# A fused attention and expert layer kernel: the statistics of batches 4 to 7 and the second table move ahead of the first expert tile, and the third weight waits for batch 0

## The chip, the cores and the metric

The kernel runs on one core of one Trainium2 chip. The metric is the device time of one execution in microseconds. Three runs of the kernel before gave 274.36, 274.52 and 274.54 us, a median of 274.52 us.

## The reference, cut to what matters

Two residual layers follow one another on x, 8 batches of 512 tokens with 128 features. The first is a mixing layer with a scan over the tokens, the second a layer of 8 experts of which each token takes 2.

```python
# layer 1
n = layernorm(x)                                  # per token, over 128 features
inp = mix * n + (1 - mix) * shifted(n)            # shifted by one token in the batch
h = relu(inp @ W_in.T + b_in)
state = state * decay + h_t                       # over the 512 tokens of a batch
x = x + layernorm(states @ W_out.T + b_out)
# layer 2
n = layernorm(x)
weights, chosen = top_k(n @ gate_kernel, 2); weights = softmax(weights)
# for each of the two (token, expert) pairs, weights w0, w1 (128 x 512), wo (512 x 128):
y = (silu(n @ w0[e]) * (n @ w1[e])) @ wo[e]
x = x + layernorm(sum of the two weighted y)
```

## The kernel before, in words

The program is written out by hand, one instruction stream for each engine, with semaphores between them; the order in each function is the order on that engine, and each engine and each DMA queue works in order. Times below are counted from the start of the profiled span.

**The head.** Batches 0, 1, 2 (and the first part of 3) go through layer 1 before the first expert tile. For batch b: `start1(b)` takes mean and variance of the raw x on DVE (`bn_stats` L953, `bn_aggr` L937), `root1(b)` the square root on ACT, `scale_z(b)` scales the projected rows on DVE; `mix_and_turn(b)` and `times_folded(b)` are matmuls, `relu(b)` is on ACT (L686), `scan(b)` on DVE (L1001), `times_w_out(b)` on PE (L1710 and L1715). `squares2(b)` and `root2(b)` on ACT give the second normalisation, `residual(b)` (L1016) on DVE the new x. Then `top`, `choice` and `choose` pick the experts on DVE, `squares(b)` and `root3(b)` on ACT and `offset3(b)` on DVE normalise, `ranks(b)` on PE and `put(b)`, `tags(b)` on DVE work out where each row goes. `normalise3(b)` on ACT (L699) writes the rows, and POOL sends them into the `expert_rows` table in DRAM by eight indirect DMAs for a batch (L524). `s_sent[0]` counts the landings of batch 0's eight.

**Tables.** `table_start(p)`, `table_end(p)`, `use_tiles(p)` on DVE make the list of tiles of phase p from the counts of the batches so far. Phase 0 holds tiles 0 to 2, phase 1 tiles 3 to 7, phase 2 tiles 8 to 15. SP loads the rows of the tiles (L370) once the table of the phase is there and the sends of its batches have landed; phase 0 needs batch 0 and the first two sends of batch 1.

**Slots.** From there one loop `for k, s, t in slots()` runs on PE, ACT, DVE and POOL. PE's slot t turns the rows of tile t (L1759), does the first two layers of tile t-1 (L1764, 16 matmul records) and the last layer of tile t-2 (L1801, 8 records). ACT copies the turned rows (L743), applies silu (L748), copies w0 for the next tile (L766) and scales the result (L777). DVE multiplies into `sb_gated` (L1368) and copies w1 for the next tile (L1387). POOL sends results to `pair_rows` (L537). The layer 1 work of batches 3 to 7 is spread over the slots; a batch takes eight. The function `batch_at(t, ahead)` says which.

**What the change touches in the slots.** Before, batches 5 to 7 get their statistics in the slots: four `bn_stats` each in DVE's slots 5, 6, 7 (`rest_sums`, L983), twelve `bn_aggr` in slot 8 (`rest_mean_var`, L990), then `rest_power` on POOL in slot 8 (two operations, L487 and L491) and `rest_means` on ACT in slot 9 (L639), which waits for the `bn_aggr`. Batch 4's are in DVE's head (`start1(4)`, after `tags(2)`). The table of phase 1 is made in DVE's slots 0 to 2, that of phase 2 in slots 2 to 4.

**SP's queue** holds in order: the loads of x and its turned copy, `load_w(0)`, `load_w(1)` (2 MB each, L340), `load_x(4, 4, B)` (1 MB, L336), the load of wo (2 MB, L362), then the tile loads. All of these travel in one DMA queue.

**Fills.** `fill(bank, n)` issues n bf16 matmuls of 128x512 (L1810) whose result nobody reads; the kernel before has them at the very start and just ahead of tile 0.

## Time and profile before

| | |
|---|---|
| median of three runs | 274.52 us (274.36 to 274.54) |
| the profiled execution's own time | 274.19 us |
| its span | 272.4 us, so 1.8 us lie around it |
| PE busy | 243.0 us, 89% |
| DVE, ACT, POOL busy | 68%, 66%, 61% |
| mean granted TensorE clock | 0.964 of full speed |

The profile was taken in one execution. A row of the timeline has the start, the duration, the engine, the line, what is written from what, how many instructions were merged into it, and in square brackets the idle time of the engine just before it with what ended it. Matmuls overlap in their pipeline, so durations of neighbours overlap.

### The profile page before, as it was taken

Reading aid. Unit: us, or ns where it says so; the run is one execution under the profiler, and the core shown is the slowest. Engines: PE = TensorE matmul, PEld = TensorE weight load, DVE = VectorE, ACT = ScalarE, POOL = GpSimd, SP = SyncE. Lnnn points to the kernel's source line nnn. Section 1 sums busy time; section 2 is a strip of 40 time slices with the busy share of each in tenths; the row PEclk is TensorE's granted clock in tenths of the full one; section 3 lists DMA queues with packets and bytes.
Section 4 is the critical chain, followed back from the end, with each engine's and each line's share of the span. In section 5 each row is a group of like instructions: output and inputs, shape, how many; then the busy total and the mean of one; then the engine's idle time right before and its main releaser. Section 6 shows DMA issues by size and latency. Waiting matters only on the chain.

```text
span 272.4 us, 8097 instructions
## 1 busy us (share of the span) xinstructions
PE 243.0 (89%) x2059; PEld 231.2 (85%) x2059; DVE 186.1 (68%) x815; ACT 179.0 (66%) x517; POOL 167.2 (61%) x190
## 2 busy tenths in 40 slices
PE   7948778899898999999999999999999999999800
PEld 2738655799898999999999999999999999999700
DVE  4886876877785785687578687844353434998774
ACT  2185869577576777785867587655656566568581
POOL 3317774773678878778878878776333324277740
PEclk9997799999999999999999999999999999999955
DMA  5999961413301321132123113433322108403048
GB/s 174 300 358 375 292 215 51 101 52 84 106 32 49 88 84 40 62 96 65 40 71 101 49 45 108 110 90 89 82 78 70 51 28 331 178 16 96 13 152 231
DMA packets 29675, 31.70 MB, mean 116 GB/s; under 512 B 4778, under 2 KB 22188, under 8 KB 29504
## 3 DMA queue, kind: packets, MB, share of 16 engines
q1 hardware_dynamic: 24448, 22.56, 27.7%
q0 software_dynamic: 4320, 8.50, 8.9%
q8 instruction: 19, 0.31, 0.5%
q10 hardware_dynamic: 864, 0.13, 0.3%
q14 instruction: 24, 0.20, 0.2%
HBM read 19.58 MB, written 12.05 MB: 116 GB/s over the span
## 4 chain that ended last, share of the span: by engine, by line
PE 73%; DVE 14%; issue 4%; POOL 4%; ACT 2%; DVEq 1%; POOLq 0%
PE bank L1764 40%; PE bank L1801 21%; PE bank L1715 3%; PE bank L1759 2%; DVE sb_early L1001 2%; PE bank L1810 2%; PE bank L1665 1%; POOL expert_rows L524 1%; ACT sb_square L653 1%; DVE sb_w_now L1387 1%; DVEq L1381 1%; DVE sb_rest_stats L983 1%; PE bank L1683 1%; POOL pair_rows L537 1%; DVE sb_x L1016 1%
## 5 line engine op out<-in xcount | busy, mean ns | idle before, releaser
L1764 PE MATMUL bank<-sb_xeT,sb_w_now 128*128 128x128 f32 x1136 | 139.5, 275 | 2.9 <-DVE sb_gated L1368 2.4
L1764 PEld LDWEIGHTS bank<-sb_xeT,sb_w_now 128*128 128x128 f32 x1136 | 133.0, 192 | 3.8 <-issue 3.8
L537 POOL DMA_INDIRECT pair_rows<-sb_y_rows,sb_y_pair x71 | 73.4, 1033 | 53.3 <-ACT sb_y_rows L777 32.3
L1368 DVE TENSOR_TENSOR sb_gated<-bank,sb_silu 128x512 f32<-128x512 f32 x71 | 48.9, 689 | 58.0 <-PE bank L1764 46.8
L524 POOL DMA_INDIRECT expert_rows<-sb_row,sb_place x64 | 64.8, 1012 | 28.9 <-issue 18.1
L1801 PE MATMUL bank<-sb_w_raw,sb_gated 128*128 x568 | 75.7, 276 | 0.4 <-ACT sb_y_rows L777 0.3
L1801 PEld LDWEIGHTS bank<-sb_w_raw,sb_gated 128*128 128x128 f32 x568 | 69.1, 192 | 1.0 <-issue 0.9
L748 ACT ACTIVATE sb_silu<-bank 128x512 f32<-128x512 f32 x71 | 42.3, 595 | 17.2 <-PE bank L1764 16.9
L743 ACT ACTIVATE sb_xeT<-bank 128x128 f32<-128x128 f32 x71 | 19.4, 274 | 40.8 <-PE bank L1759 40.5
L766 ACT ACTIVATE sb_w_now<-sb_w_raw 128x512 f32 x71 | 44.3, 624 | 0.0
L1387 DVE COPY sb_w_now<-sb_w_raw 128x512 f32 x71 | 30.2, 425 | 1.6 <-issue 1.6
L777 ACT ACTIVATE sb_y_rows<-bank,sb_y_weight 128x128 f32<-128x128 f32 x71 | 25.7, 361 | 2.0 <-PE bank L1801 1.8
L1759 PE MATMUL bank<-sb_ident_wide,sb_taken_rows 128*128 128x128 f32 x71 | 19.6, 277 | 1.4 <-ACT sb_xeT L743 1.0
L699 ACT ACTIVATE sb_row<-sb_x,sb_nm,sb_rs 128x128 f32<-128x128 f32 x32 | 14.1, 484 | 1.0 <-DVE sb_nm L1028 1.0
L1715 PE MATMUL bank<-sb_w_out_wide,sb_early 128*128 128x136 f32 x64 | 11.3, 328 | 2.7 <-DVE sb_early L1001 2.6
L1715 PEld LDWEIGHTS bank<-sb_w_out_wide,sb_early 128*128 128x128 f32 x64 | 9.6, 223 | 4.4 <-DVE sb_early L1001 4.2
L1016 DVE SCALAR_TENSOR_TENSOR sb_x<-bank,sb_rs,sb_x 128x136 f32<-128x136 f32 x32 | 9.3, 352 | 5.0 <-POOL sb_rs L482 4.9
L1759 PEld LDWEIGHTS bank<-sb_ident_wide,sb_taken_rows 128*128 128x128 f32 x71 | 10.1, 143 | 2.3 <-ACT sb_xeT L743 1.5
L482 POOL TENSOR_TENSOR sb_rs<-sb_sd,sb_minus_half 128x4 f32<-128x4 f32 x10 | 11.2, 1120 | 0.8
L1665 PE MATMUL bank<-sb_wide,sb_pairs_early 128*128 128x136 f32 x64 | 10.4, 314 | 0.0
L1665 PEld LDWEIGHTS bank<-sb_wide,sb_pairs_early 128*128 128x128 f32 x64 | 9.7, 225 | 0.7 <-ACT sb_wide L605 0.7
L1810 PE MATMUL bank<-sb_ones_b 128*128 128x512 bf16 x22 | 7.6, 495 | 2.6 <-POOL sb_pad_row L461 1.8
(203 smaller groups left out, 249.8 us busy)
## 6 DMA issues: line engine op xcount, KB each, us to landing
sb_taken_rows<-expert_rows SPq DMA_DIRECT2D x71, 65.5 KB, 1.9
sb_w_raw<-in_L_ffn_w SPq DMA_DIRECT2D x2, 2048.0 KB, 16.2
sb_pairs_early<-pair_rows SPq DMA_DIRECT2D x3, 1024.0 KB, 7.2
...
pair_rows<-sb_y_rows,sb_y_pair POOLq DMA_INDIRECT x71, 2.4
...
```

What stands on the lines that cost most here:

```text
L524: pool.indirect_dma_start(expert_rows[:, :], bass.IndirectOffsetOnAxis(ap=place[b % ROWS][:, k, j:j + 1], axis=0), row[b % ROWS][:, j, :], ...
L537: pool.indirect_dma_start(pair_rows[:, :], bass.IndirectOffsetOnAxis(ap=y_pair[group % 2][:, t % PAIRS:t % PAIRS + 1], axis=0), y_rows[slo ...
L748: act.activation(silu[t % 2][:], p_l1[:], ACT.Silu).then_inc(c["silu"], 1)
L766: act.activation(w0_now[t % 2][:].rearrange("p (c f) -> p c f", f=D), w_raw_chunks[:, bass.ds(chunks[t], FC), :], ACT.Copy).then_inc(c["w0 ...
L777: act.activation(y_rows[t % Y_SLOTS][:], p_y[t % 2][:, 0:D], ACT.Copy, scale=y_weight[group % 2][:, t % PAIRS:t % PAIRS + 1]).then_inc(c[" ...
L1368: dve.tensor_tensor(gated[t % 2][:], p_l2[:], silu[t % 2][:], ALU.mult).then_inc(c["gated"], 1)
L1387: dve.tensor_copy(w1_now[t % 2][:].rearrange("p (c f) -> p c f", f=D), w_raw_chunks[:, bass.ds(chunks[t] + W_CHUNKS, FC), :]).then_inc(c[" ...
L1665: last = pe.matmul(p_z(b)[h][:, j * Z_WIDE:(j + 1) * Z_WIDE], x_turned[:, at:at + P], wide[:, D:], start=True, stop=True)
L1715: last = pe.matmul(p_attn(b, j), states[b % 2][:, j * P:(j + 1) * P], w_out_wide[:], start=False, stop=(j % (G // 2) == 1))
L1759: pe.transpose(p_xeT, taken_rows[:, t % RING, 0:D], ident).then_inc(c["xeT_ps"], 1)
L1764: last = pe.matmul(to[:, n * P:(n + 1) * P], w[:, n * P:(n + 1) * P], x, start=True, stop=True)
L1801: last = pe.matmul(p_y[t % 2][:, 0:D], gated[t % 2][:, n * P:(n + 1) * P], wo.rearrange("p o d -> p (o d)"), start=(n == 0), stop=(n == FC ...
```

## The change

The load of x for batches 4 to 7 goes ahead of w0 and w1. SP's load of wo waits until all of batch 0's sends have landed. On DVE, `scan(0)` goes ahead of `start1(1)`, `start1(4)` moves up to between `choose(1)` and `offset3(1)`, all statistics of batches 5 to 7 and batch 4's inverse root move ahead of `residual(2)`, and the table of phase 1 is made whole ahead of the slots. The inverse roots of batches 5 to 7 are made by a square root on ACT and a reciprocal on DVE in place of POOL's two operations. ACT's order is changed around tile 0, and PE gets fills in three more places of the head.

```diff
@@ sync
             load_turned(4, 4, B)
+            load_x(4, 4, B)
             load_w(0, w0_in)
             load_w(1, w1_in)
-            load_x(4, 4, B)
+            sp.wait_ge(s_sent[0], 16 * K * G)
             sp.dma_start(w_raw[:, 2 * WCOLS:].rearrange("p (e c n) -> p e c n", e=E, c=FC),
...
@@ gpsimd
-            def rest_power():
...
-                if t == STEP:
-                    rest_power()
@@ scalar
+            def rest_root():
+                act.wait_ge(rest["mv"], 1)
+                act.activation(rest_sd[:], rest_mv[:, :, 1], ACT.Sqrt,
+                               bias=eps[:]).then_inc(rest["sd"], 1)
...
             root2(1)
             keep_z(3)
+            mean_of_x(2)
+            mean_of_x(3)
             relu(2)
...
-            mean_of_x(2)
+            root1(4)
+            mean_of_x(4)
             squares2(2)
             root2(2)
             keep_z(6)
-            relu(3)
+            keep_z(7)
+            chunk_of(0)
+            fetch_w0(0)
+            rest_root()
             squares(2, 0, G)
             root3(2)
-            keep_z(7)
-            root1(4)
-            mean_of_x(3)
-            mean_of_x(4)
             act.activation(unused[:], eps[:], ACT.Silu)
-            chunk_of(0)
-            fetch_w0(0)
+            relu(3)
+            normalise3(2, 0, G // 2)
...
                 if t == 0:
-                    normalise3(2, 0, G)
+                    normalise3(2, G // 2, G)
@@ vector
+            def rest_inverse():
+                dve.wait_ge(rest["sd"], 1)
+                dve.reciprocal(rest_rs[:], rest_sd[:]).then_inc(rest["rs"], 1)
...
             decays()
-            start1(1)
             folded_weights()
             scan(0)
+            start1(1)
...
             choose(1)
+            start1(4)
             offset3(1)
...
             use_tiles(0)
+            rest_sums(0, (B - REST) * G)
+            rest_mean_var()
+            inverse(1, 4, REST, sd1, rs1)
             residual(2)
             top(2)
             choice(2)
             choose(2)
+            rest_inverse()
             offset3(2)
             put(2)
             tags(2)
-            start1(4)
-            inverse(1, 4, REST, sd1, rs1)
             chunk_of(0)
             fetch_w1(0)
+            table_start(1)
+            table_end(1)
+            use_tiles(1)
 
             for k, s, t in slots():
-                if t == 0:
-                    table_start(1)
-                elif t == 1:
-                    table_end(1)
-                elif t == 2:
-                    use_tiles(1)
+                if t == 1:
                     table_start(2)
...
-                if t in (STEP - 3, STEP - 2, STEP - 1):
-                    rest_sums((t - STEP + 3) * G, (t - STEP + 4) * G)
-                elif t == STEP:
-                    rest_mean_var()
@@ tensor
             times_folded(2)
+            fill(bank[4], 6)
             ranks(0)
+            pe.wait_ge(a["hidden"], 2)
+            fill(bank[5], 5)
             times_w_out(1)
...
             times_folded(5)
+            pe.wait_ge(a["hidden"], 3)
+            fill(bank[5], 4)
             times_w_out(2)
             times_folded(6)
+            times_folded(7)
             mix_and_turn(3)
-            times_folded(7)
             ranks(2)
```

**SP, at the loads of x and the weights**, as a difference between the two orders. The first two rows are loads of the turned x, the row with `in_L_ffn_w` the two weights.

```order
 L345 DMA sb_pairs_early<-in_x_turned 128x512
 L345 DMA sb_pairs_early<-in_x_turned 128x2048
+L336 DMA sb_x<-in_L_attn_x 128x16x128
 L340 DMA sb_w_raw<-in_L_ffn_w 128x8x512 x2
-L336 DMA sb_x<-in_L_attn_x 128x16x128
```

The 1 MB of x now stands ahead of 4 MB of weights, and behind them comes wo with its new wait.

**DVE, between the end of `use_tiles(0)` and the choice of batch 2**, before:

```order
L1176 TENSOR_TENSOR sb_used<-sb_used,sb_take 128x8
L945 RECIPROCAL sb_rs_0<-sb_sd_0 128x4
L1016 SCALAR_TENSOR_TENSOR sb_x<-bank,sb_rs_0,sb_x 128x136 x4
L1036 MAX sb_top_0<-sb_x 128x8 x4
L1043 MAX_INDEX sb_choice_0<-sb_top_0,sb_x 128x8 x4
```

and with the change:

```order
L1178 TENSOR_TENSOR sb_used<-sb_used,sb_take 128x8
L979 BN_STATS sb_rest_stats<-sb_x 128x6 x12
L986 BN_AGGR sb_rest_mv<-sb_rest_stats 128x2 x12
L941 RECIPROCAL sb_rs_4<-sb_sd_4 128x4
L941 RECIPROCAL sb_rs_0<-sb_sd_0 128x4
L1018 SCALAR_TENSOR_TENSOR sb_x<-bank,sb_rs_0,sb_x 128x136 x4
L1038 MAX sb_top_0<-sb_x 128x8 x4
L1045 MAX_INDEX sb_choice_0<-sb_top_0,sb_x 128x8 x4
```

Twenty-four statistics and a reciprocal now stand ahead of `residual(2)`.

**DVE, from the w1 copy of tile 0 to the first product**, with the change (the six rows of `table_start` and five of `table_end` and the three of `use_tiles`, L1172 to L1178, stand above this piece):

```order
L1178 TENSOR_TENSOR sb_used<-sb_used,sb_take 128x8
L1383 TENSOR_LOAD sb_tile_chunk_i
L1383 ISA x2
L1389 ISA
L1389 COPY sb_w_now<-sb_w_raw 128x512
L1003 SCALAR_TENSOR_TENSOR sb_early<-sb_decay_row,sb_early 128x512
L1119 TENSOR_SCALAR sb_tiles_i<-sb_count_i 128x8
L1123 TENSOR_SCALAR sb_full<-sb_tiles_i 128x8
L1126 TENSOR_TENSOR sb_avail<-sb_full,sb_used 128x8
L1131 SCALAR_TENSOR_TENSOR sb_ends<-sb_ones_f,sb_avail 128x8
L1136 SCALAR_TENSOR_TENSOR sb_skip<-sb_used,sb_full 128x8
L1140 TENSOR_TENSOR sb_past<-sb_tile_f,sb_ends 128x8x8
```

Between the scan of batch 3 (L1003) and tile 0's product stands now the start of the table of phase 2; before it was the end of the table of phase 1.

## Rows read from the trace of the kernel before

**Rows 1.** Busy time by stretch: PE, PEld, DVE, ACT, POOL, then clock, DMA share, GB/s.

```profile
47.40:74.90 27.50, 25.19 (x218) 24.08 (x218) 21.50 (x106) 17.50 (x51) 17.39 (x20) 1.00 0.33 87
74.90:99.40 24.50, 23.60 (x212) 23.08 (x211) 17.67 (x75) 18.73 (x55) 19.76 (x21) 1.00 0.22 65
99.40:123.70 24.30, 24.30 (x223) 24.21 (x223) 17.39 (x76) 18.29 (x54) 19.45 (x21) 1.00 0.23 67
```

**Rows 2.** Timeline of PE, 50 to 86.5 us: the rows with an idle time before them.

```profile
50.83 1.13 PE L1764 MATMUL bank<-sb_xeT,sb_w_now 128*128 128x128 f32 x8 [0.52 <-ACT sb_silu L748]
52.75 1.13 PE L1764 MATMUL bank<-sb_xeT,sb_w_now 128*128 128x128 f32 x8 [0.79 <-DVE sb_gated L1368]
...
68.59 1.13 PE L1764 MATMUL bank<-sb_xeT,sb_w_now 128*128 128x128 f32 x8 [0.69 <-DVE sb_gated L1368]
74.33 1.15 PE L1801 MATMUL bank<-sb_w_raw,sb_gated 128*128 x8 [0.30 <-ACT sb_y_rows L777]
...
85.99 0.68 PE L1764 MATMUL bank<-sb_xeT,sb_w_now 128*128 128x128 f32 x4 [0.90 <-DVE sb_gated L1368]
```

**Rows 3.** Groups by line on DVE and POOL, 60 to 76 us: the moved and removed work.

```profile
L983 DVE BATCH_NORM_STATS2 sb_rest_stats<-sb_x 128x6 f32<-128x128 f32 x12 | 2.6, 275 | 0.0
L990 DVE BATCH_NORM_AGGREGATE sb_rest_mv<-sb_rest_stats 128x2 f32<-128x6 f32 x12 | 0.9, 148 | 0.0
...
L491 POOL TENSOR_TENSOR sb_rest_rs<-sb_rest_sd,sb_minus_half 128x12 f32<-128x12 f32 x1 | 2.3, 2297 | 0.1
```

**Rows 4.** Timeline of DVE, the start of the head.

```profile
9.41 0.87 DVE L953 BATCH_NORM_STATS2 sb_stats<-sb_x 128x6 f32<-128x128 f32 x4
10.42 0.38 DVE L937 BATCH_NORM_AGGREGATE sb_mv<-sb_stats 128x2 f32<-128x6 f32 x4
...
15.32 0.36 DVE L1016 SCALAR_TENSOR_TENSOR sb_x<-bank,sb_rs,sb_x 128x136 f32<-128x136 f32 x1
```

**Rows 5.** Timeline of PE, 9 to 43 us.

```profile
10.00 1.09 PE L1665 MATMUL bank<-sb_wide,sb_pairs_early 128*128 128x136 f32 x8
...
12.37 1.19 PE L1715 MATMUL bank<-sb_w_out_wide,sb_early 128*128 128x136 f32 x8
...
20.93 2.18 PE L1715 MATMUL bank<-sb_w_out_wide,sb_early 128*128 128x136 f32 x8 [1.60 <-DVE sb_early L1001]
...
42.09 0.33 PE L1759 MATMUL bank<-sb_ident_wide,sb_taken_rows 128*128 128x128 f32 x1 [0.36 <-DMA sb_taken_rows<-expert_rows]
```

**Rows 6.** Busy time by stretch in the head, columns as in rows 1.

```profile
17.50:20.90 3.40, 0.76 (x9) 0.42 (x9) 3.06 (x18) 3.02 (x12) 0.08 (x1) 0.99 1.03 396
20.90:24.30 3.40, 3.37 (x15) 3.37 (x16) 1.94 (x11) 1.48 (x10) 2.79 (x3) 0.51 1.05 390
```

**Rows 7.** Timeline of DVE, 27 to 52 us: the rows that end a wait, and the products.

```profile
28.88 0.18 DVE L945 RECIPROCAL sb_rs<-sb_sd 128x4 f32<-128x4 f32 x1 [0.81 <-ACT sb_sd L629]
34.64 0.18 DVE L945 RECIPROCAL sb_rs<-sb_sd 128x4 f32<-128x4 f32 x1 [0.67 <-ACT sb_sd L624]
38.80 0.18 DVE L945 RECIPROCAL sb_rs<-sb_sd 128x4 f32<-128x4 f32 x1 [0.76 <-ACT sb_sd L629]
41.43 0.18 DVE L945 RECIPROCAL sb_rs<-sb_sd 128x4 f32<-128x4 f32 x1 [0.37 <-ACT sb_sd L600]
42.67 0.43 DVE L1387 COPY sb_w_now<-sb_w_raw 128x512 f32 x1 [1.06 <-issue]
47.32 0.69 DVE L1368 TENSOR_TENSOR sb_gated<-bank,sb_silu 128x512 f32<-128x512 f32 x1 [0.44 <-issue]
51.91 0.69 DVE L1368 TENSOR_TENSOR sb_gated<-bank,sb_silu 128x512 f32<-128x512 f32 x1 [0.51 <-issue]
```

**Rows 8.** Issues of SP from the timeline: start, time in the issue.

```profile
18.88 8.60 SPq L362 DMA_DIRECT2D sb_w_raw<-in_L_ffn_wo  x1
...
39.06 2.62 SPq L370 DMA_DIRECT2D sb_taken_rows<-expert_rows  x3
```

**Rows 9.** The sends (L524): landing times of the eight issued from 20 to 31 us.

```profile
DMA to landing us min/median/max: 5.8/6.4/7.2
```

12 lines of the change are left out of this document (3 added, 9 removed).

## The prediction

> **What bounds the kernel now.** I read the page's busy shares first (in the table above): PE is the engine to watch, at 89%. Then the busy time by stretch [rows 1]. From 99.4 to 123.7 us, a batch period of eight tiles, PE is busy for all of its 24.3 us: from there to the end of the tiles the matmuls alone set the pace, and nothing the change does can be felt. The period before it has 0.9 us in which PE does nothing (24.50 less 23.60), and the stretch from the first product at 47.4 us has 2.3 (27.50 less 25.19). The timeline of PE names these gaps [rows 2]: 0.52 and 0.79 us at 51 and 53 us, 0.69 at 69, 0.30 at 74 and 0.90 at 86. They add up to 3.2 us, and that is all there is to win in the slots. Anything else must come out of the head, and the head can be judged by one moment: when PE can start the second half of tile 2's layers, at 52.75 us, released by DVE's product of tile 1 at 51.91 us [rows 2, 7].
>
> **What the change wins in the slots.** The gaps at 69 and 74 us lie in slots 7 to 9, where DVE does the twelve `bn_stats` and `bn_aggr` (2.6 and 0.9 us) and ACT waits for them. The gap at 86 us hangs on POOL: its power of 12 columns takes 2.3 us [rows 3] and pushes the sends of batch 3 and, behind them, the inverse root that `residual(4)` needs. With all of this gone, these slots hold what the later periods hold, and there PE has no gap [rows 1]. I take the three as won whole: 0.69 + 0.30 + 0.90 = **1.89 us**. The gaps at 51 and 53 us belong to the first tiles and go into the next sum.
>
> **What it costs in the head.** I follow DVE, step by step, as shifts against the times of before.
>
> First, `start1(1)` behind `scan(0)`. `start1(1)` fills a time, from 9.41 us on, in which DVE waits for the folded weights from PE anyway; now DVE stands idle there and ends the scan about half a microsecond earlier, near 11.8 us. PE gets next to nothing from it, since the projections of batch 1 hold it until 10.00 + 1.09 us and the bias product follows [rows 5]. But `start1(1)` (0.87 + 0.38 us, with the pause between them 1.39) [rows 4], its round trip over ACT, the scaling and `start1(2)` now stand in one row between the scan and `residual(0)`. I add them up to 16.1 us for that residual, which was at 15.32 [rows 4]: batch 0 comes **0.8 us later**, and POOL's first send with it.
>
> Second, the fills. From 17.5 to 20.9 us PE is busy for 0.76 of 3.40 us, and in the stretch behind the granted clock is 0.51, the 1.2 GHz level [rows 6]; there the eight `times_w_out(1)` records take 2.18 us, against 1.19 us for batch 0's at 2.4 GHz [rows 5]. The change puts 11 fills around `ranks(0)`, all in time in which PE would wait for DVE, so they cost nothing themselves. If the clock stays up, 0.99 us come back: batch 1's residual is then **0.2 us earlier** than before. The same happened again at 31 us, but behind the new order nothing waits for batch 2's product.
>
> The Trainium skill, "TensorE: Matmul & The Clock Gate", Part 1, says the array sits at 1.2 GHz after idleness and gets 2.4 GHz only after sustained activity; the rows of these two stretches agree with it. The rule also speaks against this change, since it makes PE idle elsewhere.
>
> For with `ranks(2)` late, PE idles from about 36.3 to 41.3 us, ahead of the ten fills of tile 0, and these may run at 1.2 GHz as the stretch at 20.9 us did. That costs nothing in my sum as long as the first two layers end before 50 us, so I take 0. The other end is the price of the one stretch at 1.2 GHz above, 1.0 us.
>
> Third, `start1(4)`, 1.4 us, ahead of `offset3(1)`. DVE waits there for 0.81 us anyway [rows 7]; so batch 2's scan and the first table come **0.2 us later** than before.
>
> Fourth, the statistics of batches 5 to 7 ahead of `residual(2)`: 2.6 + 0.9 us [rows 3], 0.2 for the pause and the inverse root, 3.7 us in all. Before, DVE waited 0.67 us there [rows 7]. `residual(2)` comes 0.2 + 3.7 - 0.7 = **3.2 us later**, near 38 us.
>
> Fifth, what is no longer behind it: the wait of 0.76 us for ACT at 38.80 (`relu(3)` no longer stands ahead of `squares(2)`), `start1(4)` with 1.4, and its wait of 0.37 us [rows 7]. The reciprocal of 12 columns adds 0.2. The w1 copy of tile 0 comes 3.2 - 0.8 - 1.4 - 0.4 + 0.2 = 0.8 to 0.9 us later than 42.67.
>
> Sixth, the tables. The end of the table of phase 1 and its `use_tiles` (1.5 us) now stand ahead of `scan(3)`, and the start of the next table (1.1 us) ahead of tile 0's product. So that product is late by much more, 2.7 us, near 50.0 us in place of 47.32. But the same operations are gone from between the products of tiles 0 and 1, and tile 1's comes only **1.0 us late**, at 52.9 us. The sum of operations on DVE up to there is the same; only the added statistics and the waits count.
>
> **The DMA side costs nothing in my sum.** The queue moves 396 GB/s under load [rows 6]. The 1 MB of x, now first, takes 3 us of that and lands well before DVE asks for it at 28 us; all 5 MB take 13 us from about 8 us on, and even at half the rate w1 would be there at 35 us, while it is wanted at 43. Batch 0's last send goes out near 32.4 us. The sends took 5.8 to 7.2 us to land with the weights in the way [rows 9]. Now the way may be clear, so wo starts between 33 and 39 us; I take 36. Its 2 MB take 5.3 us and a start of some 2 us. Tile 0's load, issued at 39.06 us before [rows 8] and there at 42.09 [rows 5], stands behind wo on SP and in its queue, so its rows come near 44 to 45 us. From there PE needs the turn of 0.33 us [rows 5], a copy on ACT, and two layers of about 1.0 us each [rows 2], some 2.6 us. DVE isn't ready before 50 us, so there is room for 2.5 us.
>
> **The sum.** 1.0 us lost, 1.89 won: 0.9 us less. The profiled execution took 274.19 us (span 272.4 and 1.8 around it) and would take 273.3. The median of the runs shown is 0.33 above that execution, so I forecast **273.6 us**.
>
> **The rivals.** *The head is not longer.* DVE is idle for a good part of the time from 34 to 52 us, also in the issue of its register loads (1.06, 0.44 and 0.51 us in [rows 7]), and the added 3.7 us may fall into more of it than I found. Then the product of tile 1 is at 51.9 us as before and the slots' gain stands alone: 274.52 - 1.89 = 272.6 us. For it: the chain has many short waits, and I counted four. Against: each was followed, and the additions stand in the row itself.
>
> *The clock falls all the same.* The fills leave about 1.7 us of idle time before `ranks(0)`. Then the 2.18 us stay, the 0.8 us of batch 0's delay go through, and tile 1 is 2.0 us late: 274.52 - 0.91 + 0.99 = 274.6 us, no change. Against it: PE would be busy for about twice the share that it has now.
>
> *Tile 0 waits for its rows, slower.* Place: SP, behind the load of wo. That issue held SP for 8.60 us [rows 8]. If batch 0's sends still land 6.4 us after their issue, near 38.3 us, and the issue of wo again holds the queue for 8.6 us, tile 0's load goes out at 46.9 us, its rows come 3.0 us later as now (39.06 to 42.09), and the first product is at 52.6 instead of 50.0. That is 274.52 - 0.91 + 2.6 = 276.2 us. It decides once the load's issue is later than 50.0 - 2.6 - 3.0 = 44.4 us. Against: the 8.60 us were spent with three loads queued ahead; now none is.
>
> The Trainium skill speaks for this rival. Its page "DMA: Bandwidth & Descriptors", Queues, rings and completion order, says that within a queue descriptors are taken in order, and that each engine takes turns between queues: the sends, in another queue, are then never shut out by wo, while tile 0's load is. If the wait wins nothing by that rule, the time is that of this rival or of my forecast.
>
> **How the numbers follow.** A measurement of this kernel can tell about 0.2%, 0.55 us, from no change; "faster" is below 273.97, "slower" above 275.07. Forecast (272.9 to 274.4): 0.42, three quarters of it on the fast side. Longer head absent, 272.6: 0.30. Clock falls, 274.6: 0.13, almost all within 0.2%. Rows late, 276.2, with milder forms: 0.15. Together 0.61 faster, 0.22 the same, 0.17 slower. The range 272.0 to 275.3 takes in the first three with 0.6 to 0.7 us on either side of them (most of the 1.0 us of slow fills among it) and leaves out the last.
>
> **What would show it.** Right: no gap on PE from 54 to 100 us, the stretch of tiles 9 to 16 fully busy; tile 1's product near 52.9 us; `residual(2)` near 38 us; a clock of 1.0 at 20.9 to 24.3 us; tile 0's rows landing before 47 us. Wrong: a tile load issued after 44.4 us with PE waiting on a DMA; `residual(0)` not later than 15.5 us; or gaps that stay at 69 and 86 us, which would mean that others than the moved operations caused them.

## The result, and the profile after

| | before | after |
|---|---|---|
| median of the runs, us | 274.53 (274.36 to 274.75, 4 runs) | 271.49 (270.91 to 272.23, 4 runs) |
| ratio to before | 1 | 0.989, 95% interval 0.9869 to 0.9912 |
| profiled execution, us | 274.19 | 272.23 |
| its span, us | 272.4 | 270.5 |
| product of tile 0 / 1 / 2 / 8 / 16, us | 47.32 / 51.91 / 54.78 / 74.88 / 99.31 | 50.07 / 52.87 / 55.71 / 72.94 / 97.24 |

The change takes 3.0 us off; the forecast was 0.9, and 271.49 lies below the range that I gave (272.0). The profiled executions differ by less than the medians, 1.96 us, because that of before was shorter than all the four runs beside it, and that of after the longest of its four. Of all runs reported below, three of e12_split_stats, its profiled one among them, lie more than 1.5% above its fastest; its ratio and median leave them out.

I start with DVE, on which my sum for the head was made. Timeline of DVE in the changed kernel; the columns are start, time, instruction, and in brackets the idle time before it with its releaser.

```profile
16.02 1.16 DVE L1018 SCALAR_TENSOR_TENSOR sb_x<-bank,sb_rs,sb_x 128x136 f32<-128x136 f32 x4
...
25.47 1.16 DVE L1018 SCALAR_TENSOR_TENSOR sb_x<-bank,sb_rs,sb_x 128x136 f32<-128x136 f32 x4
...
34.87 2.40 DVE L979 BATCH_NORM_STATS2 sb_rest_stats<-sb_x 128x6 f32<-128x128 f32 x12
37.31 0.91 DVE L986 BATCH_NORM_AGGREGATE sb_rest_mv<-sb_rest_stats 128x2 f32<-128x6 f32 x12
38.52 1.16 DVE L1018 SCALAR_TENSOR_TENSOR sb_x<-bank,sb_rs,sb_x 128x136 f32<-128x136 f32 x4
...
43.75 0.43 DVE L1389 COPY sb_w_now<-sb_w_raw 128x512 f32 x1 [0.75 <-issue]
...
50.07 0.69 DVE L1370 TENSOR_TENSOR sb_gated<-bank,sb_silu 128x512 f32<-128x512 f32 x1 [0.49 <-issue]
...
52.87 0.69 DVE L1370 TENSOR_TENSOR sb_gated<-bank,sb_silu 128x512 f32<-128x512 f32 x1 [0.45 <-PE bank L1763]
```

The residuals of batches 0, 1 and 2 stand at 16.02, 25.47 and 38.52 us (I had 16.1, 24.6 and about 38), the products of tiles 0 and 1 at 50.07 and 52.87 (50.0 and 52.9). The head ended where I had it. One thing is new: tile 1's product is released by PE (L1763), where in the kernel before DVE itself was late [rows 7].

Busy time by stretch, from tile 0's product to tile 8's, to tile 16's, to tile 24's; columns as in [rows 1].

```profile
50.10:73.00 22.90, 22.90 (x211) 22.81 (x210) 16.93 (x73) 17.55 (x51) 15.03 (x16) 1.00 0.32 88
73.00:97.30 24.30, 24.30 (x223) 24.21 (x222) 17.55 (x75) 18.42 (x54) 19.45 (x21) 1.00 0.22 65
97.30:121.60 24.30, 24.30 (x223) 24.21 (x222) 17.57 (x76) 18.43 (x55) 19.45 (x21) 1.00 0.25 68
```

PE has no gap left in the first two stretches. The first eight tiles take 22.9 us where they took 27.5, the next eight 24.3 where they took 24.5 [rows 1]: 4.8 us won behind tile 0's product, against 2.75 us lost ahead of it.

The granted clock of the head, by stretch of the same view:

```profile
16.30:19.70 3.40, 1.36 (x13) 0.58 (x12) 2.90 (x22) 2.16 (x12) 0.00 (x0) 1.00 1.00 303
19.70:23.10 3.40, 3.40 (x13) 1.96 (x13) 3.09 (x16) 2.24 (x7) 1.27 (x2) 0.50 1.04 393
...
29.90:33.30 3.40, 3.40 (x14) 2.15 (x13) 3.23 (x18) 3.03 (x10) 2.79 (x3) 0.50 0.16 53
...
40.20:43.60 3.40, 1.83 (x11) 0.92 (x12) 2.27 (x20) 3.34 (x11) 1.96 (x3) 0.50 1.04 323
43.60:47.00 3.40, 3.40 (x10) 1.24 (x8) 2.43 (x15) 1.19 (x5) 1.62 (x2) 0.50 0.45 115
```

Here I was wrong: despite the fills the clock went to the 1.2 GHz level at 19.7 us, as it had at 20.9 [rows 6], again from 29.9, and again from 40.2 to 47.0. The timeline of PE shows what that did ahead of tile 0:

```profile
41.77 0.19 PE L1725 MATMUL bank<-sb_taken,sb_ones_b 128*128 128x8 bf16 x1 [4.50 <-DVE sb_taken L1064]
...
42.18 4.43 PE L1809 MATMUL bank<-sb_ones_b 128*128 128x512 bf16 x10
46.40 0.42 PE L1758 MATMUL bank<-sb_ident_wide,sb_taken_rows 128*128 128x128 f32 x1
...
47.47 1.95 PE L1763 MATMUL bank<-sb_xeT,sb_w_now 128*128 128x128 f32 x16
```

The ten fills took 4.43 us; tile 0's turn followed at 46.40, its two layers ran at 2.4 GHz from 47.47 to 49.42. That is hardly before DVE was ready: where PE sets the product of tile 0 (e3 and e6 below) it starts 0.11 us after the layers end, so here PE would have allowed it at 49.5 us, and DVE took it at 50.07.

### The profile page after: what moved, and what is told of

The parts are those of the page before. It is cut to its first block, busy times and chain, and to the rows that moved or that the text cites. A ratio compares the mean times of both kernels' runs of the same rounds, so it can differ in the third digit from the quotient of the medians.

```text
span 270.5 us, 8129 instructions
## 1 busy us (share of the span) xinstructions
PE 245.0 (91%) x2074; PEld 231.1 (85%) x2074; DVE 186.3 (69%) x816; ACT 179.2 (66%) x518; POOL 167.1 (62%) x188
## 4 chain that ended last, share of the span: by engine, by line
PE 81%; DVE 13%; issue 2%; ACT 1%; POOL 1%; DVEq 0%; POOLq 0%
PE bank L1763 45%; PE bank L1800 23%; PE bank L1809 4%; PE bank L1758 3%; PE bank L1714 2%; DVE sb_x L1018 1%; DVE sb_stats L949 1%; DVE sb_early L1003 1%; DVE sb_rest_stats L979 1%; DVE sb_choice L1045 1%; DVE sb_x L1469 1%; PE bank L1690 1%; DVE sb_early L1459 1%; PE bank L1709 1%; DVE sb_x L961 1%
## 5 line engine op out<-in xcount | busy, mean ns | idle before, releaser
L1763 PE MATMUL bank<-sb_xeT,sb_w_now 128*128 128x128 f32 x1136 | 138.7, 275 | 0.2 <-DVE sb_gated L1370 0.2
L1763 PEld LDWEIGHTS bank<-sb_xeT,sb_w_now 128*128 128x128 f32 x1136 | 132.8, 192 | 0.4 <-issue 0.4
L528 POOL DMA_INDIRECT pair_rows<-sb_y_rows,sb_y_pair x71 | 74.7, 1052 | 54.2 <-ACT sb_y_rows L771 34.6
L737 ACT ACTIVATE sb_xeT<-bank 128x128 f32<-128x128 f32 x71 | 19.5, 275 | 46.1 <-PE bank L1758 45.8
L1758 PE MATMUL bank<-sb_ident_wide,sb_taken_rows 128*128 128x128 f32 x71 | 19.7, 277 | 0.0
L1809 PE MATMUL bank<-sb_ones_b 128*128 128x512 bf16 x37 | 15.3, 574 | 1.8 <-POOL sb_pad_row L462 1.8
L1809 PEld LDWEIGHTS bank<-sb_ones_b 128*128 128x128 bf16 x37 | 4.7, 134 | 7.9 <-issue 5.5
L1714 PE MATMUL bank<-sb_w_out_wide,sb_early 128*128 128x136 f32 x64 | 9.7, 299 | 0.0
L1003 DVE TENSOR_TENSOR_SCAN sb_early<-sb_decay_row,sb_early 128x512 f32<-128x512 f32 x8 | 9.7, 1214 | 0.0
```

The costliest lines, as they stand in the source:

```text
L528: pool.indirect_dma_start(pair_rows[:, :], bass.IndirectOffsetOnAxis(ap=y_pair[group % 2][:, t % PAIRS:t % PAIRS + 1], axis=0), y_rows[slo ...
L1714: last = pe.matmul(p_attn(b, j), states[b % 2][:, j * P:(j + 1) * P], w_out_wide[:], start=False, stop=(j % (G // 2) == 1))
L1758: pe.transpose(p_xeT, taken_rows[:, t % RING, 0:D], ident).then_inc(c["xeT_ps"], 1)
L1763: last = pe.matmul(to[:, n * P:(n + 1) * P], w[:, n * P:(n + 1) * P], x, start=True, stop=True)
L1809: pe.matmul(bank[:], ones_b[:], ones_b[:, None, :].broadcast_to([P, FC, P]), start=True, stop=True)
```

## The experiments

The experiments are fifteen variants and a repetition of the changed kernel, on four chips, with runs of the kernel before on the same chip. Across chips the ratio is the measure, since the median of before was 275.07 us on the first (e1 to e4), 274.45 on the second (e5 to e8), 274.57 on the third (e9, e11, e12, e14) and 274.23 on the fourth (after_again, e10, e13, e15). "P0", "P2" and "P16" are the starts of the products of tiles 0, 2 and 16 in the profiled execution, from the timeline of DVE. P0 says how long the head was, P0 to P2 what the first table did in the slots, and P2 to P16 what the statistics did. The 5.97 us of e3, e7 and e8 in P0 to P2 go with a low clock in tile 0's layers.

| kernel | median | ratio (95%) | P0 | P0 to P2 | P2 to P16 |
|---|---|---|---|---|---|
| before | 274.53 | 1 | 47.32 | 7.46 | 44.53 |
| after | 271.49 | 0.9890 (0.9869 to 0.9912) | 50.07 | 5.64 | 41.53 |
| after_again | 271.37 | 0.9899 (0.9874 to 0.9923) | 49.65 | 5.64 | 41.42 |
| e1_no_fills | 272.65 | 0.9902 (0.9868 to 0.9936) | 51.53 | 5.64 | 41.51 |
| e2_wo_at_once | 271.23 | 0.9851 (0.9808 to 0.9894) | 49.73 | 5.63 | 41.44 |
| e3_stats_in_slots | 275.92 | 1.0031 (1.0004 to 1.0057) | 49.58 | 5.97 | 44.94 |
| e4_no_stats | 270.73 | 0.9835 (0.9794 to 0.9875) | 47.11 | 7.46 | 41.21 |
| e5_start1_first | 270.56 | 0.9865 (0.9834 to 0.9896) | 48.60 | 5.63 | 41.43 |
| e6_table_in_slots | 271.96 | 0.9912 (0.9883 to 0.9941) | 48.70 | 7.56 | 41.21 |
| e7_few_fills | 272.96 | 0.9954 (0.9925 to 0.9983) | 51.08 | 5.97 | 41.73 |
| e8_fills_ahead | 272.93 | 0.9963 (0.9938 to 0.9987) | 49.48 | 5.97 | 41.74 |
| e9_before_fills | 273.52 | 0.9963 (0.9945 to 0.9981) | 46.12 | 7.31 | 44.82 |
| e10_before_dma | 275.71 | 1.0054 (1.0027 to 1.0081) | 48.64 | 7.46 | 44.62 |
| e11_slots_wo_at_once | 271.97 | 0.9915 (0.9899 to 0.9932) | 46.51 | 5.63 | 44.64 |
| e12_split_stats | 273.89 | 0.9969 (0.9939 to 0.9999) | 50.75 | 6.55 | 42.90 |
| e13_split_first_once | 269.69 | 0.9832 (0.9808 to 0.9856) | 46.95 | 5.70 | 42.36 |
| e14_first_once | 270.20 | 0.9840 (0.9822 to 0.9859) | 48.12 | 5.64 | 41.21 |
| e15_fills_both | 272.48 | 0.9923 (0.9895 to 0.9951) | 48.88 | 5.64 | 41.20 |

The runs of one kernel spread over 0.6 to 1.4 us in after, e2, e5, e11, e13 and e14 (four to six runs each), and over 3.5 to 4.1 us in e7, e8, e10 and e12 (nine to twelve runs), whose profiles all show PE idle for 1.5 to 3.3 us right ahead of tile 0. That the one causes the other is not shown: e3 has 2.89 us of the same idle time and its twelve runs spread over 1.7 us.

### What the statistics cost in the slots

e4 is the kernel before without the statistics of batches 5 to 7; their mean and inverse root are set to 0 and 1 at the start, so that part of the result is left out.

```diff
+            dve.memset(rest_mv[:], 0.0).then_inc(rest["mv"], 1)
+            dve.memset(rest_rs[:], 1.0).then_inc(rest["rs"], 1)
...
-                if t == STEP:
-                    rest_power()
...
-                if t in (STEP - 3, STEP - 2, STEP - 1):
-                    rest_sums((t - STEP + 3) * G, (t - STEP + 4) * G)
-                elif t == STEP:
-                    rest_mean_var()
```

> The kernel before with the statistics of batches 5 to 7 left out: constants (mean 0, inverse root 1) are set at the start, and the bn_stats, bn_aggr and the power on POOL are gone. It prices the slots' gaps alone. If the page's idle times are their price: 274.5 - 1.9 = 272.6 us. If the weight loads' idle times are (0.85, 0.30, 0.50, 1.07 and some small ones, 2.7 to 3.2 us): 271.3 to 271.8 us.

The profiled execution took 270.7 us, 3.5 less than that of before, with nearly the same head (P0 at 47.11). P2 to P16 is 3.3 us shorter. So the statistics cost 3.3 us where they stood, not the 1.89 that I read off PE's gaps. By medians on its chip e4 is 4.3 us faster (270.73 against 275.07); where the last 1 us comes from no profile here shows. Busy time by stretch of e4, from tile 0's product to tile 8's and to tile 16's:

```profile
47.10:71.50 24.40, 23.07 (x207) 22.61 (x206) 18.57 (x82) 17.58 (x52) 16.92 (x18) 1.00 0.37 96
71.50:95.80 24.30, 24.30 (x223) 24.21 (x223) 17.44 (x75) 18.42 (x54) 19.46 (x21) 1.00 0.23 68
```

The gaps left in the first stretch are those of the table, at 50 and 52 us.

e3 puts the statistics back into slots 5 to 8 of the changed kernel, with POOL's power in slot 8, and takes `rest_root` and `rest_inverse` out of the head:

```diff
-            rest_sums(0, (B - REST) * G)
-            rest_mean_var()
             inverse(1, 4, REST, sd1, rs1)
...
+                if t in (STEP - 3, STEP - 2, STEP - 1):
+                    rest_sums((t - STEP + 3) * G, (t - STEP + 4) * G)
+                elif t == STEP:
+                    rest_mean_var()
```

> The changed kernel with the statistics of batches 5 to 7 back in slots 5 to 8 of DVE and their power back on POOL. Theory A (three gaps of PE worth 2.9 to 3.2 us, against 3.7 us of DVE in the head that cost some 2.5 to 3): the gaps at 69, 74 and 86 us are back, tile 1's product is 2 to 3 us earlier, total 271.0 to 272.5 us. Theory B (the move of the statistics is the gain): 273.5 to 274.5 us.

It is slower than the kernel before, above the ranges of both theories. P2 to P16 is 44.94 us, 3.4 more than in the changed kernel, nearly the same price as in e4. But DVE's head, 3.4 us shorter (done at 46.2 us, where the changed kernel's was at 49.6), brought P0 forward by only 0.5 us, to 49.58. Timelines of DVE and PE in e3:

```profile
49.58 0.69 DVE L1381 TENSOR_TENSOR sb_gated<-bank,sb_silu 128x512 f32<-128x512 f32 x1 [3.38 <-PE bank L1775]
```

```profile
45.32 0.47 PE L1770 MATMUL bank<-sb_ident_wide,sb_taken_rows 128*128 128x128 f32 x1 [2.89 <-DMA sb_taken_rows<-expert_rows]
```

DVE stood idle for 3.38 us, since tile 0's rows landed only at 45.3 us and the clock was low in its layers (2.81 us, in place of 1.95). That is the wait of my third rival, hidden in the changed kernel by the long head.

### The wait of wo, and tile 0's rows

e2 is the changed kernel without the wait; e11 is e3 without it.

```diff
-            sp.wait_ge(s_sent[0], 16 * K * G)
             sp.dma_start(w_raw[:, 2 * WCOLS:]...
```

> The changed kernel, with wo's load issued behind w1 and no wait. Theory A: tile 0 is held by DVE and PE, not by its rows, so 271.3 to 271.8 us; batch 0's sends land 3 to 4 us later, tile 0's load goes out near 40 us all the same. Theory B (the wait for the sends gives the gain): 272.5 us or more, PE or ACT waiting on the rows of tile 0 or 3.

> The changed kernel with the statistics of batches 5 to 7 back in slots 5 to 8 and the load of wo without its wait. With the wait that kernel took 275.9 us, its tile 0 was turned at 45.3 us when its rows landed, and the product came at 49.6 us although DVE was done at 46.2. Theory A (the wait puts wo's 2 MB in the queue right ahead of tile 0's rows, and these are the limit once DVE's head is short): rows land before 43.5 us, product of tile 0 at 46.5 to 48 us, time 1.5 to 3 us less than with the wait, ratio to before 0.992 to 0.998. Theory B (the rows land late because of the sends and of the slow clock, whatever wo does): turn again at 45 us or later, ratio 1.002 as before.

e2 shows no difference that could be told from the changed kernel (0.9851 against 0.9890, intervals overlapping; profiled executions 272.0 and 272.23). e11 took 271.97 us, 3.9 us less than e3 by medians (on another chip) and 3.2 by ratios. Timelines of PE in e11, and of SP in e3 and in e11 (the load of tile 0 opens the row that names it):

```profile
42.05 0.42 PE L1769 MATMUL bank<-sb_ident_wide,sb_taken_rows 128*128 128x128 f32 x1
```

```profile
33.75 0.72 SPq L363 DMA_DIRECT2D sb_w_raw<-in_L_ffn_wo  x1
39.63 1.53 SPq L371 DMA_DIRECT2D sb_taken_rows<-expert_rows  x2
```

```profile
16.89 3.22 SPq L362 DMA_DIRECT2D sb_w_raw<-in_L_ffn_wo  x1
38.66 2.62 SPq L370 DMA_DIRECT2D sb_taken_rows<-expert_rows  x3
```

With wo at 16.89 us tile 0's load goes out at 38.66 and its rows are turned at 42.05, at most 3.4 us later (the fills still ran until then; in the kernel before it was 3.0, from 39.06 to 42.09 [rows 5, 8]). With wo at 33.75 the load goes out 1.0 us later and the rows take 5.7 us. P0 moves from 49.58 to 46.51, where it is DVE's again. So the wait costs 3.1 us up to P0 as soon as DVE's head does not cover it. The Trainium skill, "DMA: Bandwidth & Descriptors", section "Queues, rings and completion order", says that each DMA engine takes a ring's descriptors in order. The traces fit it: the rows take 5.7 us behind wo's 2 MB against 3.0 to 3.4 without, and from 38 to 44 us the core's DMA moves 308 to 332 GB/s in e3 and 64 to 112 in e11. That the order delays the rows, and not just the sharing of the DMA engines with wo, no run here separates.

e2 and e11 differ in the statistics alone, so they price that move where the wait is out of the way. P0 is 49.73 us in e2 and 46.51 in e11, P2 to P16 41.44 and 44.64, and the product of tile 16 stands at 96.80 and 96.78 us: in these two profiles the head pays the 3.2 us that the slots win. The clock was low near 20 us in e2 only, which is worth nearly 1 us (below); by medians the move wins 0.7 us, by ratios 1.7, on different chips. The 4.4 us between e3 and the changed kernel are for the most part the price of the wait. e11, which has the rest of the change, is already at 0.9915.

e10 makes the change's DMA part alone in the kernel before.

```diff
+            load_x(4, 4, B)
             load_w(0, w0_in)
             load_w(1, w1_in)
-            load_x(4, 4, B)
+            sp.wait_ge(s_sent[0], 16 * K * G)
```

> The kernel before with the change's DMA part alone: x of batches 5 to 7 first, wo held back until batch 0's sends have landed. Theory A (wo's 2 MB then stand ahead of tile 0's rows, and DVE's short head has no cover for them): rows of tile 0 land at 44 to 45.5 us instead of 42.1, product of tile 0 at 48.5 to 49.5 instead of 47.3, time 1.0 to 2.5 us more, ratio 1.004 to 1.009. Theory B (the sends land sooner with the way clear, and tile 0's load goes out as much earlier): no difference, ratio 0.999 to 1.001.

Slower by 1.5 us (1.0054), as theory A had it (the x that moves is that of batches 4 to 7): the rows came at 44.10 us in place of 42.09 [rows 5], P0 at 48.64.

```profile
44.10 0.33 PE L1760 MATMUL bank<-sb_ident_wide,sb_taken_rows 128*128 128x128 f32 x1 [2.48 <-DMA sb_taken_rows<-expert_rows]
```

So the wait of wo is a part of the change that hurts by itself and is neutral only behind the longer head. The new place of the load of x stays in e11, where the rows come at most 3.4 us after the issue of their load, so it is the wait and not that place.

### The table, and start1(1)

e6 puts the first new table back into slots 0 to 2; e5 puts `start1(1)` ahead of `folded_weights()` and `scan(0)` again.

```diff
-            table_start(1)
-            table_end(1)
-            use_tiles(1)
...
-                if t == 1:
+                if t == 0:
+                    table_start(1)
+                elif t == 1:
+                    table_end(1)
+                elif t == 2:
+                    use_tiles(1)
```

> The changed kernel with the end of the first new table and its start back in slots 0 to 2, as before the change; the statistics stay in front of tile 0. Theory A (PE is not free before tile 0's turn, 46.4 us, and DVE has the same work up to tile 1's product in either order): product of tile 0 near 49.6 us instead of 50.1, tile 1's at 53 to 54 us with PE gaps of 0.5 and 0.8 us again in front of the second layers as the kernel before has them at 51 and 53 us; time 0 to 1 us above the changed kernel, ratio to before 0.989 to 0.993. Theory B (the move of the table is itself what won more than I had counted): over 1.5 us above the changed kernel, ratio 0.995 or more.

P0 to P2 is 7.56 instead of 5.64 us: the table costs 1.9 us in the slots. In the head it is nearly free, for P0 in e6 is not up to DVE. The timeline of DVE:

```profile
48.70 0.69 DVE L1370 TENSOR_TENSOR sb_gated<-bank,sb_silu 128x512 f32<-128x512 f32 x1 [1.57 <-PE bank L1765]
```

DVE was ready 1.57 us before PE's layers of tile 0, which wait for the rows and the turn (45.53 us). The table fills this time; it is 1.9 us won that way against 0.2 lost (P0 48.88 in e15, whose clock fell and rose as in e6 up to 38 us). The profiled executions of e6 and e15 took 272.58 and 270.87 us. In medians e6 has 271.96 us against 271.49 and 271.37 for the changed kernel, within theory A's 0 to 1 us; the intervals of the ratios overlap, so that the table's gain is shown by the products, not by the times.

```diff
+            start1(1)
             folded_weights()
             scan(0)
-            start1(1)
```

> The changed kernel with start1(1) back ahead of the folded weights on DVE, as before the change. Theory A (my step one was right, DVE's chain in the head passes its delay on): residual(0) returns from 16.0 to 15.3 us and POOL's first send from 21.5 to 20.8; of these 0.7 us some 0.2 to 0.7 reach the product of tile 1 (52.9 us in the changed kernel), so 0.2 to 0.7 us less than the changed kernel, ratio to before 0.986 to 0.988. Theory B (batch 1's residual waits for PE's product of w_out and ACT's root in either order, and swallows the 0.7 us): no difference from the changed kernel, ratio 0.989.

270.56 us, 0.8 to 0.9 below the changed kernel by medians (0.9865 against 0.9890 and 0.9899, so the intervals overlap); P0 48.60. `residual(0)` is at 15.46, 0.56 us earlier than in the changed kernel (0.30 earlier than in after_again, where it is at 15.76). I read it as theory A: the move of `start1(1)` is another part that seems to hurt. But P0 is 1.5 us earlier, and 0.9 of that goes with the clock, the next point; against e15, whose clock also stayed up near 20 us, P0 is only 0.3 us earlier.

### The fills and the clock

e9 is the kernel before with the three new groups of fills alone, e1 the changed kernel without them.

```diff
+            fill(bank[4], 6)
             ranks(0)
+            pe.wait_ge(a["hidden"], 2)
+            fill(bank[5], 5)
             times_w_out(1)
...
+            pe.wait_ge(a["hidden"], 3)
+            fill(bank[5], 4)
             times_w_out(2)
```

> The kernel before with the change's three groups of fills (15 matmuls) and their waits alone. Theory A (my step two: the clock stays up and batch 1's product of w_out takes 1.19 instead of 2.18 us): the granted clock is 1.0 from 20.9 to 24.3 us, residual(1) comes 0.5 to 1.0 us earlier and the time is 0.3 to 1.0 us less, ratio 0.996 to 0.999. Theory B (as the changed kernel's profile shows, the clock falls for one stretch all the same, only where it falls moves): no difference, ratio 0.999 to 1.001, and a stretch at 0.5 lies again between 17 and 32 us.

> The changed kernel without its three new groups of fills (15 matmuls). Theory A (the gain is the moved statistics, and the clock dips of the head come with the fills as without): same as the changed kernel, 271.3 to 271.8 us. Theory B (the fills win a good part): 272.5 to 273.5 us, with the granted clock at 1.2 GHz for more of the head than with them.

e9 is faster, 1.0 us (0.9963), and just as my step two had it. Busy time by stretch, the residuals on DVE, and then `residual(1)` in the kernel before:

```profile
20.70:24.10 3.40, 3.40 (x26) 3.04 (x27) 2.54 (x14) 2.24 (x13) 2.79 (x3) 1.00 1.05 386
36.70:40.10 3.40, 3.40 (x9) 0.93 (x7) 1.82 (x12) 1.88 (x5) 2.75 (x3) 0.51 0.43 140
```

```profile
15.01 1.16 DVE L1016 SCALAR_TENSOR_TENSOR sb_x<-bank,sb_rs,sb_x 128x136 f32<-128x136 f32 x4
23.57 1.16 DVE L1016 SCALAR_TENSOR_TENSOR sb_x<-bank,sb_rs,sb_x 128x136 f32<-128x136 f32 x4
```

```profile
24.86 1.16 DVE L1016 SCALAR_TENSOR_TENSOR sb_x<-bank,sb_rs,sb_x 128x136 f32<-128x136 f32 x4
```

The clock stays up over batch 1's product of w_out, and `residual(1)` comes at 23.57 instead of 24.86; the clock falls later, at 36.7 us, with the ten fills ahead of tile 0. In the changed kernel the same fills do this in some executions only. Its two profiled ones had the clock at 0.50 and 0.51 in the stretches from 19.7 and from 19.1 us, and e7, the same kernel up to there, at 0.54 from 19.7; e6, e8 and e15, also the same up to there, had it at 1.00. From `residual(0)` to `residual(1)` is 9.45 us in the changed kernel and 8.57 in e15, so this fall costs 0.9 us. Ahead of `ranks(0)` PE still idles for 2.04 us in the changed kernel. Of the eight profiled executions with this idle time (2.04 or 2.05 us) the clock fell in four (after, after_again, e2, e7) and stayed up in four (e6, e8, e11, e15); of the four with 1.37 or 1.38 us (e5, e9, e13, e14, all with `start1(1)` first) it fell in none. So a part of what the clock gave e5 may be owed to `start1(1)` too; four executions are too few to show it. Without the fills (e1) P0 is at 51.53. Its median lies in theory B's range, 1.2 us above the changed kernel, but on another chip, and by ratios the two can't be told apart.

e7 has 2 fills instead of 10 ahead of tile 0's turn, e8 has 16 ahead of `ranks(2)` and 2 behind, e15 has 16 ahead and the ten behind.

```diff
             ranks(2)
             pe.wait_ge(a["z_kept"], B - 2)
-            fill(p_l1, 10)
+            fill(p_l1, 2)
```

> The changed kernel with 2 instead of 10 fills on PE ahead of tile 0's turn; in the changed kernel these ten ran at the 1.2 GHz level, took 4.43 us, and the turn stood behind them at 46.40 us. Theory A (the slow fills hold up tile 0): the turn comes as soon as the rows are there, near 44.5 us, the product of tile 0 is then up to DVE at 49.5 us instead of 50.1, and the time is 0.3 to 0.6 us less than that of the changed kernel, ratio to before 0.987. Theory B (the fills buy the clock for tiles 0 and 1): the first layers run at the 1.2 GHz level, 16 weight loads near 3.8 instead of 1.9 us, the product of tile 1 is 1 to 2 us later, and the time is 1 to 2 us above the changed kernel, ratio 0.993 to 0.996.

```diff
-            ranks(2)
             pe.wait_ge(a["z_kept"], B - 2)
-            fill(p_l1, 10)
+            fill(p_l1, 16)
+            ranks(2)
+            fill(p_l1, 2)
```

(in e15 the last line is `fill(p_l1, 10)`)

> The changed kernel with 16 fills ahead of ranks(2), where PE stands idle from 37.3 to 41.8 us, and only 2 between ranks(2) and tile 0's turn. Theory A (PE idle of 4.5 us is what lets the clock fall, and the slow fills behind it hold up tile 0): the granted clock stays at 1.0 from 41 us on, the turn of tile 0 comes near 44.5 us, product of tile 0 near 49.5 us, 0.3 to 0.6 us less than the changed kernel, ratio to before 0.987. Theory B (the clock level near tile 0 costs nothing, DVE alone sets it): no difference from the changed kernel, ratio 0.989, with product of tile 0 at 50.0 us.

> The changed kernel with 16 more fills ahead of ranks(2), in PE's idle time from 37.3 us on, and the ten behind it kept. Theory A (the clock stays up, so the ten fills take 2.3 instead of 4.4 us; but tile 0 waits for its rows until 46 us and DVE until 49.5 anyway): no difference to within 0.4 us, ratio 0.988 to 0.991. Theory B (with the clock up, turn, copy and first layers come sooner, product of tile 0 at 49.4 instead of 50.1 us): 0.5 to 0.8 us less, ratio 0.986 to 0.987.

My idea in e7 was wrong: the turn did not come sooner, since the rows weren't there before 46.1 us, and the low clock went on into the layers, 3.51 us for their sixteen matmuls in place of 1.95. Timeline of PE in e7:

```profile
46.12 0.48 PE L1758 MATMUL bank<-sb_ident_wide,sb_taken_rows 128*128 128x128 f32 x1 [2.84 <-DMA sb_taken_rows<-expert_rows]
...
47.46 3.51 PE L1763 MATMUL bank<-sb_xeT,sb_w_now 128*128 128x128 f32 x16
```

By medians it cost 1.5 us. e8 cost as much, and neither of its theories holds: the clock stayed up to 41.8 us, but the rows landed only at 44.8, PE idled for 3.32 us ahead of the turn, the clock fell there, and the sixteen matmuls took 3.23 us. In e15 PE has no long idle stretch and the clock stays up from 31.8 us on:

```profile
40.20:43.60 3.40, 2.69 (x17) 1.20 (x17) 2.25 (x16) 3.22 (x7) 1.08 (x2) 1.00 1.02 311
43.60:47.00 3.40, 2.07 (x15) 1.59 (x16) 2.68 (x13) 1.80 (x6) 2.50 (x3) 1.00 0.32 78
```

P0 is at 48.88 us and set by DVE ([0.49 <-issue] stands before it, as in the changed kernel), so the turn's delay by the slow fills costs nothing there as long as the clock is up when the layers begin. e15's median is 272.48, 1.1 us above the changed kernel on the same chip, with runs from 270.81 to 273.40. Its profile is one of the shortest (270.87) and doesn't show why; PE idles for 1.44 us ahead of the turn in it, which the ten slow fills would have covered, so the clock may fall into the layers in other executions. The clock is at most a part of it, since a run of 271.35 us and one of 272.85 have the same mean granted clock, 0.970. The time, 0.9923, is outside the ranges of both my theories, and its cause stays open.

### Towards a better kernel

e14 is the changed kernel with `start1(1)` first and wo at once. e12 and e13 leave only batch 5's statistics in the head; those of batches 6 and 7 go to DVE's slots 9 and 11, their inverse roots to POOL in slot 12. e13 has e14's two edits as well.

```diff
-            rest_sums(0, (B - REST) * G)
-            rest_mean_var()
+            rest_sums(0, G)
+            rest_mean_var(0, G)
...
+                if t == STEP + 1:
+                    rest_sums(G, 2 * G)
+                elif t == STEP + 3:
+                    rest_sums(2 * G, 3 * G)
+                    rest_mean_var(G, 3 * G)
...
+                if t == STEP + 4:
+                    rest_power()
```

> The changed kernel with start1(1) ahead of the folded weights, and the load of wo without its wait. Each alone gave 270.6 and 271.2 us against 271.5. Theory A (start1(1) is worth 0.7 us on DVE's head, and the wait of wo nothing): as start1(1) ahead alone, ratio 0.986. Theory B (both shorten the way of tile 0, the rows being near the limit): 0.2 to 0.5 us less still, ratio 0.984 to 0.985.

> The changed kernel with only batch 5's statistics in front of tile 0; those of batches 6 and 7 stand in slots 9 and 11 on DVE, their inverse roots on POOL in slot 12. Theory A (each of the statistics costs its duration on DVE's head, and PE-bound slots take them for nothing): DVE's head is 2.0 to 2.4 us shorter, product of tile 0 at 47.8 to 48.5 us if the rows are there, no new PE gap, time 1 to 2.4 us less than the changed kernel, ratio to before 0.980 to 0.985. Theory B (POOL, which is nearly full in the slots, passes the extra power on as the gap of 0.9 us at 86 us did, and rows land only at 46 us): no gain over the changed kernel, ratio 0.989 or more, with a PE gap near 88 to 100 us.

> The changed kernel with batch 5's statistics alone in the head (those of 6 and 7 in slots 9 to 12), start1(1) ahead of the folded weights and wo without its wait. With the wait the split took 274.3 us: its tile 0 was turned at 45.7 us on its rows, the clock was low until 51.8 us, and PE had a gap of 0.86 us at 95.3. Theory A (the rows alone undid it): product of tile 0 at 46 to 46.5 us, against 48.2 us without the split, time 1 to 2 us less than the 270.2 us without it, ratio 0.978 to 0.981. Theory B (POOL's power gives most of it back): the gap near 93 us is there again and the slots cost 1 to 1.5 us more, ratio 0.982 to 0.985.

> The changed kernel, unchanged, on this chip. Theory A (the gain is that of the first measurement): ratio to before 0.987 to 0.991. Theory B (the first four runs were lucky ones, the stretches at the lower clock fall otherwise in most): ratio 0.991 to 0.995, runs spread over more than 1.5 us.

after_again confirms the result (0.9899). e14 takes 270.20 us, 0.9840, as its theory B had it. e12 gains nothing over the changed kernel, also as its theory B had it; in its profiled execution, the longest of the twelve, tile 0 was turned at 45.7 us on its rows, and a PE gap of 0.86 us appeared at 95.3. e13 comes out as its own theory B says (0.9832), with P0 later than theory A's 46.5: with the rows there its head is 1.2 us shorter than e14's, and P2 to P16 gives 1.15 back. Timelines of POOL, DVE and PE in e13:

```profile
84.54 1.67 POOL L491 TENSOR_TENSOR sb_rest_rs<-sb_rest_sd,sb_minus_half 128x8 f32<-128x8 f32 x1
```

```profile
88.84 0.16 DVE L1041 SCALAR_TENSOR_TENSOR sb_nm<-sb_mv,sb_rs 128x4 f32<-128x4 f32 x1 [1.52 <-POOL sb_rs L482]
```

```profile
90.92 1.13 PE L1779 MATMUL bank<-sb_xeT,sb_w_now 128*128 128x128 f32 x8 [0.85 <-DVE sb_gated L1381]
```

POOL's power of 8 columns pushes the next batch's inverse root, DVE waits for it in front of a product, and PE for the product: the chain that made the gap at 86 us in the kernel before [rows 2]. e13 at 269.69 us (0.9832) is the best that ran, 4.5 us below the kernel before and 1.7 below the changed one on the same chip; e14 can't be told from it, and is the simpler one. The new order of ACT, the earlier `start1(4)` and the inverse roots on ACT and DVE were not tried alone.

## Why the prediction was wrong in size

**The step that failed** is the first: "I take the three as won whole: 0.69 + 0.30 + 0.90 = 1.89 us". The slots gave 3.0 us in the changed kernel (P2 to P16, 44.53 to 41.53), and e4 and e3 put the statistics' price there at 3.3 and 3.4. The mechanism was right; the term was read from the wrong row. PE's rows in the trace overlap, which I take to be why a gap between them comes out too short. The same gaps in the timeline of PEld, the weight loads, in the kernel before:

```profile
50.80 0.97 PEld L1764 LDWEIGHTS bank<-sb_xeT,sb_w_now 128*128 128x128 f32 x8 [0.73 <-issue]
52.72 0.97 PEld L1764 LDWEIGHTS bank<-sb_xeT,sb_w_now 128*128 128x128 f32 x8 [0.95 <-issue]
...
68.56 0.97 PEld L1764 LDWEIGHTS bank<-sb_xeT,sb_w_now 128*128 128x128 f32 x8 [0.85 <-issue]
...
72.83 0.99 PEld L1715 LDWEIGHTS bank<-sb_w_out_wide,sb_early 128*128 128x128 f32 x8 [0.30 <-DVE sb_early L1001]
74.33 0.97 PEld L1801 LDWEIGHTS bank<-sb_w_raw,sb_gated 128*128 128x128 f32 x8 [0.50 <-issue]
...
77.34 0.97 PEld L1801 LDWEIGHTS bank<-sb_w_raw,sb_gated 128*128 128x128 f32 x8 [0.15 <-issue]
...
85.95 0.97 PEld L1764 LDWEIGHTS bank<-sb_xeT,sb_w_now 128*128 128x128 f32 x8 [1.07 <-issue]
```

From 68 us on they add up to 0.85 + 0.30 + 0.50 + 0.15 + 1.07 = 2.87 us. The number even stood in [rows 1], which I read by its PE column: by PEld the first two stretches have 27.50 - 24.08 = 3.42 and 24.50 - 23.08 = 1.42 us without a weight load, and a full period 0.09. That makes 4.7 us for the slots, table and statistics together; 4.8 were won. The Trainium skill has this for whole kernels ("Perfetto Trace Analysis", section "Identifying the Most-Contended Engine"): the busy share of matmuls is a poor measure of how near a kernel is to its limit, because pipelined instructions look smaller in the trace, and the busy share of the weight loads is one of the two measures to use instead. With 3.0 in place of 1.89 my sum gives 272.2 us for the profiled execution, which took 272.23.

By medians I was off by 2.1 us (0.9 forecast, 3.0 measured), and the slots are 1.1 of them. The other 1.0 is not explained by a term of the sum. Of it, 0.7 is that the profiled execution was that much above its median, and 0.3 that I set the median above the profiled execution by the distance that the kernel before had.

**Head, 1.0 us at tile 1's product**: right in number, 51.91 to 52.87, with tile 0's product 2.75 us late (2.7 forecast) and the table's 1.8 us won back between the products. That it is right is in part luck, since the step on the clock inside it failed.

**The clock** over batch 1's product: wrong in the profiled execution, right in the profiles of e9, e6, e8 and e15. `residual(1)` was 0.6 us later than in the kernel before instead of 0.2 earlier, and DVE's later waits took a part of that up: `residual(2)` was half a microsecond later than I had it. The rival "the clock falls all the same" met its condition and missed its price: tile 1 was 1.0 us late, not 2.0, and batch 1's product took 1.55 us, not 2.18. An execution where the clock stays up has P0 as much as 1.2 us earlier (e15); this is what I take the rest of the gap between forecast and medians to be. The mean granted clocks of the runs fit it. Of the fifteen runs of after, after_again and e2, the five at 0.952 or 0.953, the three profiled ones among them, took 271.75 to 272.29 us, and the ten at 0.958 to 0.962 took 270.77 to 271.60. Where the clock of those ten stayed up no profile shows, so that step is argued. The rule of the Trainium skill on the clock gate that I weighed ("TensorE: Matmul & The Clock Gate", Part 1) agrees with the largest fall: that at 40.2 us comes with 4.50 us of idle time on PE, and where e15 filled most of it the clock stayed up. The falls near 20 and 30 us came with 2.04 and 1.68 us of idle time, that near 20 us in some executions only.

**DMA costs nothing**: right in this kernel, for the reason given (DVE isn't ready before 50 us), but by less than I had. Tile 0's rows were there at 46.2 us, not 44 to 45, as the timeline of PEld in the changed kernel has it:

```profile
46.20 0.18 PEld L1758 LDWEIGHTS bank<-sb_ident_wide,sb_taken_rows 128*128 128x128 f32 x1 [0.50 <-DMA sb_taken_rows<-expert_rows]
```

By my 2.6 us from rows to product 1.3 us of room was left, not 2.5, and the way took 3.2 us (46.20 to 49.42), so that only half a microsecond was left. Without the long head the wait costs 3.1 us (e3 against e11), and alone it costs 1.5 (e10). The rival named the place rightly; its mechanism, a late issue of the load, did not occur (wo's issue held SP for 0.72 us, and the load went out at 40.34 us, well ahead of 44.4): the rows themselves took longer behind wo, as the text on the DMA side had it. That rival's sum also has a slip: 32.4 + 6.4 us is 38.8 and not 38.3, so its times are 0.5 us too early.

**Chances and range**: 0.61 for faster was right in direction. The range ended at 272.0 because it took its low side from the PE gaps as a ceiling ("that is all there is to win in the slots"). That ceiling was the number to doubt.
